# A graph layer kernel: dense products with their sides swapped, hop tables gathered in two float32r parts, 16 of 25 batches dense

## The chip, the cores and the metric

The kernel runs on one core of one Trainium2 chip. The metric is the device time of one execution in microseconds. Three executions took 3998.82, 3994.66 and 3999.19 us, the median is 3998.82 us. The engines are TensorE (PE in the rows; its weight loads are PEld), VectorE (DVE), ScalarE (ACT), GpSimd (POOL) and SyncE (SP, which here only issues transfers). They run at once and wait for each other through semaphores. A row such as L1175 names line 1175 of the kernel.

## The reference

There are 12500 nodes of 128 features and 212500 edges, sorted by destination: 100000 random pairs in both directions and a loop on each node.

```python
h = relu(layernorm(x))                            # per node
msg = where(edge_type == 0, h[src] @ W_data.T + b_data, h[src] @ W_control.T + b_control)
x = x + relu(segment_sum(msg, dst) + h @ W_self.T + b_self)
h = relu(layernorm(x))
norm = deg_inv_sqrt[src] * deg_inv_sqrt[dst]      # deg = edges into a node
y = h; total = h
for _ in range(2):                                # two hops
    y = segment_sum(y[src] * norm[:, None], dst)
    total = total + y
return x + total / 3
```

## The kernel before

**Nodes and edges.** The nodes are 98 blocks of 128, four blocks are a batch (512 nodes), so there are 25 batches. The edges are 208 groups of 8 chunks of 128 edges.

**The typed pass (k = 0).** A first stage makes a table of both kinds of messages for each node. Then the pass goes over all 208 groups. For each chunk GpSimd gathers 128 rows from the table in HBM (`gather`, L874), and VectorE makes a one-hot matrix of the destinations of the group (`make_hot`, L1465). TensorE multiplies both in fp32 (`sum_rows`, L1091), and VectorE adds the 128 rows of sums into a window of seven node blocks, in two parts where they straddle two blocks (`add_group`, L1487). When a batch is complete it is finished (`finish`): residual, layernorm, and the scaled rows that the first hop reads. They are stored as a table of fp32 rows of 512 bytes in HBM (`store_nodes`, L732). They are also kept in SBUF as two float32r parts (`table_parts`): the high part is ScalarE's copy (L982), the low part is what VectorE finds missing (L1413), so both together carry the fp32 value.

Beside it the pass makes count strips: for each of the first 60 destination blocks (15 batches) a matrix of how often each source node is linked to each destination. VectorE makes one-hot matrices (L1509 and L1512), four cells of edges at a time (a quad, 480 in all), in slots 24 to 205. TensorE multiplies them (L1135), ScalarE turns the counts into uint8 (L1002), SP stores them. TensorE also runs bf16 products that nobody reads (`fill`, L1126).

**The hops (k = 1, 2).** The first 15 batches are dense: their sums are the product of the count strips with the whole table in SBUF. The rest is sparse and goes as in the typed pass, with 82 groups per hop. A hop runs over slots. In slot i TensorE sums group i, then does its share of the dense steps (`dense_step`). A step is one tile (a block of 128 destinations) by one piece of 14 source blocks. It takes 14 products with the counts as the stationary side and 256 columns of the table (high and low part side by side) as the moving side (L1175). There are 60 x 7 = 420 steps per hop. The last slots of a pass already do steps of the next hop, the lead (`LEAD_TILES`). VectorE adds the two parts of each finished tile (`read_tile`, L1542).

The counts of a step come from HBM through a ring of seven places (`load_counts`, L772). ScalarE casts them from uint8 to float32r into a ring of three strips (`cast_counts`, L1011). SP issues the load of a place when the cast that used it is done, and it works in one fixed order: the loads of the slot's steps, then reloads, then stores of the batch that leaves, then the load of a batch that comes.

Gathers go through a ring of four places of 8 chunks (`RING`). At a hop's start GpSimd waits until the whole table is stored.

At the end of hop 1 the table in SBUF is replaced by the new one. SP reads 14 pieces of 7 blocks back (`reload`, L783), each when the last step that uses it is done and its batches are stored. ScalarE and VectorE split each again (L1016, L1413).

## Time and profile before

| | |
|---|---|
| median of three executions | 3998.82 us |
| the profiled execution, first to last instruction (its span) | 3997.9 us |
| around the span, against the median | 0.9 us |
| busy in the span: PE, PEld | 3405.9 us (85%), 2729.2 us (68%) |
| busy in the span: POOL, ACT, DVE | 2879.8 us (72%), 2329.7 us (58%), 2186.3 us (55%) |
| moved in the span | 571.77 MB, mean 143 GB/s |

The profiled execution has no time of its own beside the span. The page also shows the span in 40 slices. In the slices of the typed pass PE is busy 0.7 to 0.8, DVE 0.8 and the DMA engines 0.3. In those of the hops PE is busy 0.9 or more, DVE 0.2 and the DMA engines 0.6. Shares are means over stages with different limits, so each stage is read from its own rows. Matmuls are pipelined, so the mean time of one row (285 ns) is longer than the distance from one to the next.

### The profile page before, as it was taken

The numbers are of one execution on the slowest core, as the hardware profiler recorded it, in microseconds if no ns is written. First come the engines' busy times: TensorE is split into PE (matmuls) and PEld (weight loads), VectorE is DVE, ScalarE is ACT, GpSimd is POOL, SyncE is SP. The second block draws the span as 40 slices with busy tenths as digits, with TensorE's granted clock in tenths as the row PEclk, the third lists the DMA queues.
The fourth block names the chain that finished last, engine by engine and source line by source line (L and its number), as shares of the span: only waits on it lengthen the run. The fifth ranks groups of instructions, "written<-read, shape, count | busy, mean of one in ns | idle before, by whom it ended". The sixth has DMA issues, their size and how long they took to land.

```text
span 3997.9 us, 62254 instructions
## 1 busy us (share of the span) xinstructions
PE 3405.9 (85%) x23420; PEld 2729.2 (68%) x23420; DVE 2186.3 (55%) x3333; ACT 2329.7 (58%) x3075; POOL 2879.8 (72%) x3058
## 2 busy tenths in 40 slices
PE   7666777777777787777777899999998899999999
PEld 4344444444444444444444799999998899999999
DVE  7523888888888888888888422222222222222222
ACT  4001444444444444444444688888887788888887
POOL 2677777777777777777777577777776477777775
PEclk9788998999999999999999999999999999999999
DMA  6222333333333334333333566666666666666665
GB/s 194 85 61 61 109 119 121 113 109 110 126 109 110 114 110 128 110 109 125 110 115 112 170 179 187 192 192 187 189 189 184 179 179 176 187 182 181 179 184 145
DMA packets 367268, 571.77 MB, mean 143 GB/s; under 512 B 66678, under 2 KB 308225, under 8 KB 359283
## 3 DMA queue, kind: packets, MB, share of 16 engines
q1 hardware_dynamic: 270435, 370.74, 29.6%
q0 software_dynamic: 95664, 196.60, 19.2%
q8 instruction: 188, 3.08, 0.3%
q14 instruction: 117, 0.96, 0.1%
q10 hardware_dynamic: 864, 0.39, 0.0%
HBM read 424.48 MB, written 142.99 MB: 142 GB/s over the span
## 4 chain that ended last, share of the span: by engine, by line
PE 44%; POOL 38%; issue 13%; DVE 2%; DMA 2%; ACT 1%; SPq 0%; DVEq 0%; POOLq 0%; ACTq 0%
POOL rows L874 38%; PE wide L1175 34%; PE sums_bank L1091 7%; PE wide L1056 1%; ACT strip_ring L1011 1%; DMA stage<-hop_table 1%; DMA rows<-typed_table,index 0%; PE turned_bank L1126 0%; DVE big L1214 0%; DVE rows L1254 0%; DVE stage L1512 0%; POOL stage L914 0%; PE wide L1135 0%; DMA stage<-strips 0%; DMA big<-in_x 0%
## 5 line engine op out<-in xcount | busy, mean ns | idle before, releaser
L874 POOL DMA_INDIRECT rows<-typed_table,index x1661 | 1589.0, 957 | 506.0 <-issue 505.0
L874 POOL DMA_INDIRECT rows<-hop_table,index x1306 | 1251.9, 959 | 481.4 <-issue 394.9
L1011 ACT CAST strip_ring<-stage 128x1792 fp32r<-128x1792 uint8 x840 | 1409.2, 1687 | 285.3 <-PE wide L1175 279.2
L1175 PE MATMUL wide<-table_parts,strip_ring 128*128 128x256 f32 x11760 | 1461.0, 285 | 35.7 <-ACT strip_ring L1011 35.7
L1175 PEld LDWEIGHTS wide<-table_parts,strip_ring 128*128 128x128 f32 x11760 | 1431.3, 193 | 38.0 <-ACT strip_ring L1011 17.5
L1002 ACT CAST stage<-wide 128x392 uint8<-128x392 f32 x1920 | 790.3, 502 | 983.9 <-PE wide L1135 982.6
L1126 PE MATMUL turned_bank<-all_twos 128*128 128x512 bf16 x3328 | 1112.0, 394 | 0.0
L1091 PE MATMUL sums_bank<-rows,hot 128*128 128x129 f32 (+1 forms) x5934 | 801.2, 292 | 287.0 <-DMA rows<-typed_table,index 272.6
L1091 PEld LDWEIGHTS sums_bank<-rows,hot 128*128 128x128 f32 x5934 | 764.4, 206 | 337.8 <-issue 304.0
L1512 DVE TENSOR_TENSOR stage<-count_up,stage 128x1568 bf16<-128x1568 f32 x480 | 855.4, 1782 | 0.0
L1135 PE MATMUL wide<-stage 128*128 128x392 bf16 x1920 | 652.6, 340 | 221.8 <-DVE stage L1512 220.0
L1487 DVE SCALAR_TENSOR_TENSOR sums<-sums_bank,in_upper,sums 128x129 f32 (+1 forms) x372 | 129.8, 349 | 1064.8 <-PE sums_bank L1091 1042.6
L1126 PEld LDWEIGHTS turned_bank<-all_twos 128*128 128x128 bf16 x3328 | 339.0, 102 | 344.6 <-issue 53.5
L1135 PEld LDWEIGHTS wide<-stage 128*128 128x128 bf16 x1920 | 191.9, 100 | 460.2 <-DVE stage L1512 317.5
L1465 DVE TENSOR_TENSOR hot<-count_up,local 128x1024 f32<-128x1024 f32 x372 | 451.8, 1215 | 0.1
L1509 DVE TENSOR_TENSOR stage<-count_up,stage 128x512 bf16<-128x512 f32 x480 | 328.2, 684 | 174.2 <-PE wide L1135 174.0
L1542 DVE TENSOR_REDUCE own_in<-wide 128x128 f32<-128x256 f32 x120 | 50.8, 423 | 356.9 <-PE wide L1175 356.9
L976 ACT ACTIVATE batch_spread<-batch_spread 128x8 f32<-128x8 f32 x25 | 5.4, 216 | 249.6 <-DVE batch_spread L1225 249.6
L1487 DVE SCALAR_TENSOR_TENSOR sums<-sums_bank,base_all,sums 128x129 f32 (+1 forms) x372 | 127.8, 343 | 0.4
L1056 PE MATMUL wide<-stage,rows 128*128 128x384 f32 x196 | 78.5, 528 | 0.0
L1413 DVE TENSOR_TENSOR table_parts<-stage,table_parts 128x896 fp32r<-128x896 f32 x14 | 15.3, 1092 | 73.6 <-ACT table_parts L1016 73.6
L1402 DVE SCALAR_TENSOR_TENSOR xin<-scaled,xin 128x512 f32<-128x512 f32 (+1 forms) x50 | 34.2, 684 | 37.9 <-ACT scaled L945 35.1
(141 smaller groups left out, 669.5 us busy)
## 6 DMA issues: line engine op xcount, KB each, us to landing
stage<-strips SPq DMA_DIRECT2D x840, 224.0 KB
strips<-stage SPq DMA_DIRECT2D x60, 1568.0 KB
rows<-typed_table,index POOLq DMA_INDIRECT x1661
rows<-hop_table,index POOLq DMA_INDIRECT x1306
resid<-xin SPq DMA_DIRECT2D x50, 256.0 KB, 3.0
hop_table<-scaled SPq DMA_DIRECT2D x50, 256.0 KB, 3.8
xin<-resid SPq DMA_DIRECT2D x50, 256.0 KB
typed_table<-rows SPq DMA_DIRECT2D x49, 256.0 KB, 2.1
```

What stands on the lines that cost most here:

```text
L874: pool.indirect_dma_start(out=rows[:, o % RING, c, 0:P], out_offset=None, in_=tables[k], in_offset=bass.IndirectOffsetOnAxis(ap=index[:, c ...
L1002: act.copy(count_strips[tile % 2][:, :, w * CELL:(w + 1) * CELL], wide[:, nth % CELL_BANKS, 0:real_blocks * CELL].rearrange("p (b n) -> p ...
L1011: act.copy(strip_ring[:, number % STRIP_RING], counts_ring[place]).then_inc(strip_cast, 1)
L1056: last = pe.matmul(wide[:, i % 2 * PAIR + b, 0:KINDS * P], normed_t[i % 2][:, b * P:(b + 1) * P], w_all[:, :], start=True, stop=True)
L1091: last = pe.matmul(sums_bank[:, bank, 0:columns], hots[:, c, :], rows[:, slot, c, 0:columns], start=(c == 0), stop=(c == size - 1))
L1126: pe.matmul(turned[:, 0:4 * P].rearrange("p (n f) -> p n f", n=4), all_twos[:, :], all_twos[:, :].unsqueeze(1).to_broadcast([P, 4, P]), st ...
L1135: pe.matmul(wide[:, nth % CELL_BANKS, 0:real_blocks * CELL], quad_low[quad % 2][:, w, :], quad_hot[quad % 2][:, w, :], start=True, stop=Tr ...
L1175: last = pe.matmul(wide[:, nth % 4, 0:PARTS * P], strip_ring[:, number % STRIP_RING, b - first, :], table_parts[:, b, :, :].rearrange("p n ...
L1465: dve.tensor_tensor(hot[:, place, :, :], counting(CHUNKS, P), local[:, group * CHUNKS:(group + 1) * CHUNKS].unsqueeze(2).to_broadcast([P, ...
L1487: last = dve.scalar_tensor_tensor(out=into, in0=sums_bank[:, o % 2, 0:columns], scalar=inside_tile, in1=into, op0=ALU.mult, op1=ALU.add)
L1509: dve.tensor_tensor(quad_low[place], counting(QUAD, P), cell_low[:, cells].unsqueeze(2).to_broadcast([P, QUAD, P]), ALU.is_equal)
L1512: dve.tensor_tensor(quad_hot[place], counting(QUAD, columns), cell_key[:, cells].unsqueeze(2).to_broadcast([P, QUAD, columns]), ALU.is_equ ...
```

## The change

**The sides are swapped.** A step is now one batch (four tiles) by one piece of 4 source blocks. The stationary side is one part of one table block, the moving side the counts of the four tiles, 512 columns. High and low part are two products that accumulate in the same bank, so the result is the sum of both already, but transposed: features by nodes. VectorE copies it out (`read_batch`), TensorE turns it with four transposes (`turn_batch`), and `finish` reads the turned bank. There are 25 pieces (the last has two blocks) and 400 steps per hop.

**The counts** are loaded for two steps at a time, four tiles by 8 blocks, into a ring of three such loads.

**The hop tables** hold 256 words per row, the high and the low part, and are stored by two transfers. For hop 2's table, too, ScalarE now makes the high part (into the first words of `index`) and VectorE the low part. Both wait in the queue: ScalarE's copy also waits for the table stores of the previous batch, and the store waits for `low_ready`. The gathers fetch 1 KB rows into a ring of three places. The one-hot matrices of the hops are float32r, a chunk is one product of 256 columns, and VectorE adds the two halves one after the other. The reload writes both parts straight into the SBUF table.

**16 batches are dense**: 64 tiles, 512 quads in the same slots, 73 groups per hop, the dense steps in 71 slots.

```diff
-DENSE_BATCHES = 15
+DENSE_BATCHES = 16
 DENSE_TILES = DENSE_BATCHES * NODE_BLOCKS
 PAIR_TILES = 9
 PARTS = 2
-STEP_BLOCKS = 14
-COUNT_RING = 7
+STEP_BLOCKS = 4
+LOAD_STEPS = 2
+COUNT_RING = 3
 STRIP_RING = 3
 RELOAD_BLOCKS = 7
-RELOAD_RING = 3
 RELOADS_AT_ONCE = 3
 STAGE_WORDS = 11264
-DENSE_SLOTS = 80
-LEAD_TILES = 3
-LEAD_AT_ONCE = 3
+DENSE_SLOTS = 71
+LEAD_BATCHES = 1
+LEAD_AT_ONCE = 4
...
+        strip_ring = sbuf("strip_ring", [STRIP_RING, NODE_BLOCKS, STEP_BLOCKS, P], F32R)
+        row_words = HOP_RING * CHUNKS * PARTS * P - RING * CHUNKS * TILE
+        assert STRIP_RING * piece_words + COUNT_RING * count_words + row_words <= STAGE_WORDS
+        sbuf("rest_of_stage", [STAGE_WORDS - STRIP_RING * piece_words - row_words])
+        hop_rows = sbuf("hop_rows", [HOP_RING, CHUNKS, PARTS * P], F32R)
+        hop_hot = sbuf("hop_hot", [HOT_RING, CHUNKS, P], F32R)
...
-            def store_nodes(n, k, s):
+            def store_nodes(n, k, s, even):
                 if k < HOPS:
                     sp.wait_ge(resid_ready, n + 1)
                     sp.dma_start(of_batch(resid, s), in_blocks(xin[:, n % XIN, :])).then_inc(resid_stored[n % XIN], 16)
-                    sp.wait_ge(scaled_ready, n + 1)
-                    sp.dma_start(of_batch(tables[k + 1], s), in_blocks(scaled[:, n % 2, :])).then_inc(table_stored[n % 2], 16)
+                    nodes = slice(s * BATCH, s * BATCH + held(s) * P)
+                    sp.wait_ge(low_ready, n + 1)
+                    for part, values in enumerate((high_of(k, s, even), low_of(n, k, s, even))):
+                        sp.dma_start(tables[k + 1][nodes, part * P:(part + 1) * P].rearrange("(b p) f -> p b f", p=P),
+                                     values.bitcast(F32)).then_inc(table_stored[n % 2], 16)
...
+                def load_counts(n):
+
+                    k, j = divmod(n, loads_per_hop)
+                    q, part = counts_orders[k + 1][j]
+                    covered = pieces_of_counts(part)
+                    first, end = blocks_of_piece(covered[0]).start, blocks_of_piece(covered[-1]).stop
+                    place = n % COUNT_RING
+                    if n >= COUNT_RING:
+                        sp.wait_ge(strip_cast, end_of_counts[n - COUNT_RING] + 1)
+                    sp.dma_start(counts_ring[place][:, :, 0:(end - first) * P],
+                                 strips[q * NODE_BLOCKS:(q + 1) * NODE_BLOCKS, :, first:end, :].rearrange("t p b n -> p t (b n)")
                                  ).then_inc(counts_in[place], 16)
...
+                def reload(piece):
                     for s in reload_batches(piece):
                         n = event_of[1][s]
-                        sp.wait_ge(table_stored[n % 2], 16 * count_of(n + 1, 2, n % 2))
+                        sp.wait_ge(table_stored[n % 2], 32 * count_of(n + 1, 2, n % 2))
                     sp.wait_ge(strip_used, last_step_with(piece) + 1)
-                    if r >= RELOAD_RING:
-                        sp.wait_ge(reload_low, r - RELOAD_RING + 1)
                     first = piece * RELOAD_BLOCKS
-                    sp.dma_start(in_blocks(reloaded[r % RELOAD_RING], RELOAD_BLOCKS),
+                    sp.dma_start(table_parts[:, first:first + RELOAD_BLOCKS, :, :].rearrange("p b n f -> p b (n f)").bitcast(F32),
                                  tables[2][first * P:(first + RELOAD_BLOCKS) * P, :].rearrange("(b p) f -> p b f", p=P)
-                                 ).then_inc(reload_in[r % RELOAD_RING], 16)
+                                 ).then_inc(reload_in[piece], 16)
 
                 def load_counts_behind(numbers):
                     for number in numbers:
-                        if number + COUNT_RING < HOPS * steps_per_hop:
-                            load_counts(number + COUNT_RING)
+                        n = counts_of_step[number]
+                        if number == end_of_counts[n] and n + COUNT_RING < HOPS * loads_per_hop:
+                            load_counts(n + COUNT_RING)
...
-                    pool.wait_ge(summed, o - RING + 1)
+                    pool.wait_ge(summed, o - RING + 1 if o < groups else max(groups, o - HOP_RING + 1))
...
+                if k < HOPS:
+                    blocks = held(s)
                     act.wait_ge(scaled_ready, n + 1)
-                    act.copy(table_parts[:, first:first + blocks, 0, :], in_blocks(scaled[:, n % 2, 0:blocks * P], blocks)).then_inc(high_ready, 1)
+                    if n and not (k == 0 and even):
+                        act.wait_ge(table_stored[(n - 1) % 2], 32 * count_of(n, 2, (n - 1) % 2))
+                    act.copy(high_of(k, s, even), in_blocks(scaled[:, n % 2, 0:blocks * P], blocks)).then_inc(high_ready, 1)
...
+                    n = counts_of_step[number]
+                    _, _, _, piece = step_at(number)
+                    columns = len(blocks_of_piece(piece)) * P
+                    ahead = piece % LOAD_STEPS * STEP_BLOCKS * P
+                    act.wait_ge(counts_in[n % COUNT_RING], 16 * (n // COUNT_RING + 1))
                     if number >= STRIP_RING:
                         act.wait_ge(strip_used, number - STRIP_RING + 1)
-                    act.copy(strip_ring[:, number % STRIP_RING], counts_ring[place]).then_inc(strip_cast, 1)
-
-                def part_high(r, piece):
-                    first = piece * RELOAD_BLOCKS
-                    act.wait_ge(reload_in[r % RELOAD_RING], 16 * (r // RELOAD_RING + 1))
-                    act.copy(table_parts[:, first:first + RELOAD_BLOCKS, 0, :], in_blocks(reloaded[r % RELOAD_RING], RELOAD_BLOCKS)
-                             ).then_inc(reload_high, 1)
+                    act.copy(strip_ring[:, number % STRIP_RING].rearrange("p t b n -> p t (b n)")[:, :, 0:columns],
+                             counts_ring[n % COUNT_RING][:, :, ahead:ahead + columns]).then_inc(strip_cast, 1)
...
+            def sum_rows(k, bank, slot, size, place):
+                columns = TILE if k == 0 else PARTS * P
                 for c in range(size):
-                    last = pe.matmul(sums_bank[:, bank, 0:columns], hots[:, c, :], rows[:, slot, c, 0:columns],
+                    hots, values = (hot, rows) if k == 0 else (hop_hot, hop_rows)
+                    last = pe.matmul(sums_bank[:, bank, 0:columns], hots[:, place, c, :], values[:, slot, c, 0:columns],
                                      start=(c == 0), stop=(c == size - 1))
                 return last
...
+                    for b in blocks:
+                        for part in range(PARTS):
+                            last = pe.matmul(wide[:, nth % 4, 0:BATCH].rearrange("p (t n) -> p t n", t=NODE_BLOCKS),
+                                             table_parts[:, b, part, :], strip_ring[:, number % STRIP_RING, :, b - blocks.start, :],
+                                             start=(begins and b == blocks.start and part == 0),
+                                             stop=(ends and b == blocks[-1] and part == PARTS - 1))
                     last.then_inc(strip_used, 1)
+
+                def turn_batch(k, q):
+
+                    nth = nth_product(k, q)
+                    pe.wait_ge(batch_read, nth + 1)
+                    if nth:
+                        earlier = (k, q - 1) if q else (k - 1, DENSE_BATCHES - 1)
+                        pe.wait_ge(fresh_made, event_of[earlier[0]][earlier[1]] + 1)
+                    for b in range(NODE_BLOCKS):
+                        last = pe.transpose(turned[:, b * P:(b + 1) * P], own_in[:, q % 2, b * P:(b + 1) * P], identity[:, :])
+                    last.then_inc(batch_turned, 1)
...
+                dve.wait_ge(scaled_ready, n + 1)
+                dve.wait_ge(high_ready, n + 1)
+                dve.tensor_tensor(low_of(n, k, s, even), in_blocks(values, blocks), high_of(k, s, even).bitcast(F32), ALU.subtract
+                                  ).then_inc(low_ready, 1)
...
+                    for part in range(PARTS if k else 1):
+                        if part:
+                            last.then_inc(high_added, 1)
+                            dve.wait_ge(high_added, o - groups + 1)
+                        for n, inside_tile in enumerate((in_upper[:, group:group + 1], in_lower[:, group:group + 1])):
+                            into = flat_sums[:, ds(base - tile_place(first) + n * TILE, columns)]
+                            last = dve.scalar_tensor_tensor(out=into, in0=sums_bank[:, o % 2, part * P:part * P + columns], scalar=inside_tile,
+                                                            in1=into, op0=ALU.mult, op1=ALU.add)
                     last.then_inc(added, 1)
...
+                def read_batch(k, q):
+                    nth = nth_product(k, q)
+                    dve.wait_ge(strip_used, step_number(k, batch_last[k][q]) + 1)
+                    earlier = nth_product(k, q - 2) if q >= 2 else (nth_product(k - 1, max(s for s in range(DENSE_BATCHES) if s % 2 == q % 2))
+                                                                    if k > 1 else -1)
+                    if earlier >= 0:
+                        dve.wait_ge(batch_turned, earlier + 1)
+                    dve.tensor_copy(own_in[:, q % 2, :], wide[:, nth % 4, 0:BATCH]).then_inc(batch_read, 1)
```

On TensorE, in the middle of a hop, the order before has at the border of two slots a step's products, the sum of a group from `rows` and `hot`, and the next step:

```order
L1175 MATMUL wide<-table_parts,strip_ring 128x256 [waits strip_cast]
L1175 MATMUL wide<-table_parts,strip_ring 128x256 x13
L1091 MATMUL sums_bank<-rows,hot 128x128 [waits rows_landed0,added,hot_ready]
L1091 MATMUL sums_bank<-rows,hot 128x128 x7
L1175 MATMUL wide<-table_parts,strip_ring 128x256 [waits strip_cast]
```

After the change, at such a border, with the result of a batch in `own_in` to be turned:

```order
L1217 MATMUL wide<-strip_ring,table_parts 128x512 [waits strip_cast]
L1217 MATMUL wide<-strip_ring,table_parts 128x512 x7
L1131 MATMUL sums_bank<-hop_rows,hop_hot 128x256 [waits hop_rows_landed0,added,hot_ready]
L1131 MATMUL sums_bank<-hop_rows,hop_hot 128x256 x7
L1231 MATMUL turned_bank<-identity,own_in 128x128 [waits fresh_made,batch_read]
L1231 MATMUL turned_bank<-identity,own_in 128x128 x3
L1217 MATMUL wide<-strip_ring,table_parts 128x512 [waits strip_cast]
```

A step of 14 products of 256 columns became one of 8 products of 512 columns with the names on the input side exchanged, the sum has 256 columns, and the turn stands ahead of the slot's dense steps and waits for VectorE's copy and for the finishing of the batch before it.

On SyncE, where the first reloads of hop 1's end begin, the order before is this (`stage` holds counts and reloaded rows, `strips` the counts in HBM):

```order
L772 DMA stage<-strips 128x1792 [waits strip_cast] x10
L730 DMA resid<-xin 128x4x128 [waits resid_ready]
L732 DMA hop_table<-scaled 128x4x128 [waits scaled_ready]
L772 DMA stage<-strips 128x1792 [waits strip_cast] x5
L783 DMA stage<-hop_table 128x7x128 [waits strip_used,table_stored0,table_stored1]
L783 DMA stage<-hop_table 128x7x128 [waits table_stored1,strip_used,table_stored0]
L783 DMA stage<-hop_table 128x7x128 [waits table_stored1,strip_used]
```

And after:

```order
L811 DMA stage<-strips 128x4x1024 [waits strip_cast] x3
L821 DMA table_parts<-hop_table 128x7x256 [waits strip_used,table_stored0,table_stored1]
L821 DMA table_parts<-hop_table 128x7x256 [waits table_stored1,strip_used,table_stored0]
L763 DMA resid<-xin 128x4x128 [waits resid_ready]
L767 DMA hop_table<-index 128x4x128 [waits low_ready]
L767 DMA hop_table<-scaled 128x4x128
L811 DMA stage<-strips 128x4x1024 [waits strip_cast] x3
```

The reload goes to `table_parts` with rows of 256 words, the table is stored by two transfers behind the wait for `low_ready`, and a slot sends three loads of counts where it sent five. Each reload still waits for `strip_used` ahead of the next counts.

## Rows read from the trace of the kernel before

**Rows 1.** Timeline: where the dense products of each hop begin (start, duration).

```profile
2240.74 10.31 PE L1175 MATMUL wide<-table_parts,strip_ring 128*128 128x256 f32 x84 [0.75 <-ACT strip_ring L1011]
...
3127.79 13.74 PE L1175 MATMUL wide<-table_parts,strip_ring 128*128 128x256 f32 x98 [7.07 <-ACT strip_ring L1011]
```

**Rows 2.** Stretches: length, busy (instructions) per engine, granted clock, DMA share, GB/s.

```profile
2240.70:3127.80 887.10, 859.22 (x7187) 857.98 (x7187) 233.92 (x427) 716.35 (x437) 628.37 (x653) 0.99 0.66 186
3127.80:3997.90 870.10, 855.23 (x7186) 854.53 (x7186) 212.83 (x388) 704.70 (x421) 623.58 (x653) 0.99 0.63 177
300.00:2150.00 1850.00, 1419.78 (x7795) 852.49 (x7793) 1514.49 (x2036) 805.66 (x1958) 1402.02 (x1471) 0.92 0.36 112
2400.00:3000.00 600.00, 600.00 (x5074) 600.00 (x5074) 158.75 (x287) 495.54 (x296) 455.38 (x475) 1.00 0.67 189
3045.00:3127.80 82.80, 58.99 (x444) 58.07 (x443) 28.08 (x40) 49.02 (x37) 28.59 (x28) 0.88 0.64 173
...
10.00:30.00 20.00, 14.84 (x47) 8.76 (x48) 13.81 (x55) 10.70 (x29) 0.00 (x0) 1.00 1.06 304
```

**Rows 3.** The chain that ended last, inside hop 1 (start, duration).

```profile
2604.40 1.78 PE sums_bank L1091 x16
2606.18 8.39 PE wide L1175 x70
```

**Rows 4.** Groups by form, 300 to 2150 us: busy, mean ns, idle before.

```profile
L874 POOL DMA_INDIRECT rows<-typed_table,index x1456 | 1388.5, 954 | 443.7 <-issue 442.8 <-PE sums_bank L1091 0.9
L1126 PE MATMUL turned_bank<-all_twos 128*128 128x512 bf16 x2908 | 993.0, 392 | 0.0
L1512 DVE TENSOR_TENSOR stage<-count_up,stage 128x1568 bf16<-128x1568 f32 x460 | 819.8, 1782 | 0.0
...
L1509 DVE TENSOR_TENSOR stage<-count_up,stage 128x512 bf16<-128x512 f32 x460 | 314.6, 684 | 165.1 <-PE wide L1135 164.9
...
L914 POOL DMA_INDIRECT stage<-edge_pairs,cell_first x15 | 14.4, 962 | 4.6 <-issue 4.6
...
L982 ACT CAST table_parts<-scaled 128x512 fp32r<-128x512 f32 x21 | 13.0, 617 | 28.6 <-DVE scaled L1404 28.6
...
L1153 PE MATMUL wide<-identity,stage 128*128 128x128 f32 x30 | 5.8, 277 | 0.0
```

**Rows 5.** Groups by form, both hops.

```profile
L1175 PE MATMUL wide<-table_parts,strip_ring 128*128 128x256 f32 x11760 | 1461.0, 285 | 35.7 <-ACT strip_ring L1011 35.7
...
L1011 ACT CAST strip_ring<-stage 128x1792 fp32r<-128x1792 uint8 x839 | 1407.6, 1687 | 285.3 <-PE wide L1175 279.2 <-DMA stage<-strips 6.1
L874 POOL DMA_INDIRECT rows<-hop_table,index x1306 | 1251.9, 959 | 481.4 <-issue 394.9 <-DMA hop_table<-scaled 83.5 <-PE sums_bank L1091 3.1
...
L1487 DVE SCALAR_TENSOR_TENSOR sums<-sums_bank,in_upper,sums 128x128 f32 x164 | 57.5, 351 | 862.2 <-PE sums_bank L1091 861.9 <-issue 0.3
```

**Rows 6.** Transfers issued, 2400 to 3000 us: KB each, median us to landing.

```profile
stage<-strips SPq DMA_DIRECT2D x295, 224.0 KB
rows<-hop_table,index POOLq DMA_INDIRECT x475
resid<-xin SPq DMA_DIRECT2D x17, 256.0 KB, 3.5
```

**Rows 7.** Timeline: fillers and casts one behind the other.

```profile
2229.05 3.62 PE L1126 MATMUL turned_bank<-all_twos 128*128 128x512 bf16 x16
...
2238.91 9.62 ACT L1011 CAST strip_ring<-stage 128x1792 fp32r<-128x1792 uint8 x6
```

**Rows 8.** Hop 1's end: three pieces of the chain, then a gather of the timeline.

```profile
3053.80 4.87 DMA stage<-hop_table
...
3071.41 6.20 DMA stage<-hop_table
3077.82 0.66 issue
...
3058.27 1.65 POOL L874 DMA_INDIRECT rows<-hop_table,index  x1 [0.30 <-issue]
```

More of the change, by code:

```diff
@@ L161, in gnn_kernel, with blocks_of_piece, pieces_of_counts @@
-    lead_steps, orders = zip(*([(0, [])] + [order_of_steps(k) for k in range(1, HOPS + 1)]))
-    assert all(len(orders[k]) == steps_per_hop for k in range(1, HOPS + 1))
+    pieces = -(-real_blocks // STEP_BLOCKS)
+    loads = -(-pieces // LOAD_STEPS)
+    steps_per_hop = DENSE_BATCHES * pieces
+    loads_per_hop = DENSE_BATCHES * loads
+    def blocks_of_piece(piece):
+        return range(piece * STEP_BLOCKS, min((piece + 1) * STEP_BLOCKS, real_blocks))
+    def pieces_of_counts(part):
+        return range(part * LOAD_STEPS, min((part + 1) * LOAD_STEPS, pieces))
@@ new lines, in parts_of_batch, with order_of_counts @@
+    def parts_of_batch(s):
+        return {block // (STEP_BLOCKS * LOAD_STEPS) for block in range(s * NODE_BLOCKS, min((s + 1) * NODE_BLOCKS, real_blocks))}
+    last_of_pass = [{total - 1}, {total - 1, DENSE_BATCHES - 1}]
+    def order_of_counts(k):
+        late = set().union(*(parts_of_batch(s) for s in last_of_pass[k - 1]))
+        lead = [(q, part) for q in range(LEAD_BATCHES) for part in range(loads) if part not in late]
+        order = lead + [(q, part) for q in range(LEAD_BATCHES) for part in sorted(late)]
+        order += [(q, part) for q in range(LEAD_BATCHES, DENSE_BATCHES) for part in range(loads)]
+        return sum(len(pieces_of_counts(part)) for _, part in lead), order
@@ new lines, in gnn_kernel @@
+    lead_steps, counts_orders = zip(*([(0, [])] + [order_of_counts(k) for k in range(1, HOPS + 1)]))
+    orders = [[(q, piece) for q, part in order for piece in pieces_of_counts(part)] for order in counts_orders]
+    assert all(len(orders[k]) == steps_per_hop and len(counts_orders[k]) == loads_per_hop for k in range(1, HOPS + 1))
+    counts_of_step = [n for k in range(1, HOPS + 1) for n, (_, part) in enumerate(counts_orders[k], (k - 1) * loads_per_hop)
+                      for _ in pieces_of_counts(part)]
@@ L499, in table_need @@
         def table_need(k):
[L501 removed]
+            return [32 * count_of(k * total, 2, parity) for parity in range(2)]
         def event_at(k, slot):
@@ L534, in step_at, with dense_at, nth_product @@
             return k + 1, j, *orders[k + 1][j]
-        def tiles_done_in(k, i):
-            return [t for t in range(DENSE_TILES) if tile_slot[k][t] == i]
+        def dense_at(k, slot):
+            return [s for at, s in events[k] if at == slot and is_dense(k, s)]
+        def nth_product(k, q):
+            return (k - 1) * DENSE_BATCHES + q
         TURN, PLACE, FETCH, CELLS_TURN, CELLS_AHEAD = 2, 4, 10, 2, 6
```

206 lines of the change are left out of this document (85 added, 121 removed).

## The prediction

> **What bounds the kernel now.** I read the timeline for where the parts begin, the chain of waits inside a hop, the stretches, the groups by form, the transfers, and at last the end of hop 1. The span has three parts: the typed pass up to 2240.7 us, hop 1 to 3127.8 us and hop 2 to the end [rows 1, 2]. Up to 2240.7 us GpSimd's gathers set the pace: one is 0.954 us and 0.30 us of issue follows, 1850 us hold 1456 of them and 15 of the cells' (1471 x 1.257 = 1849 us), and GpSimd waited for sums 0.9 us in all [rows 2, 4]. In the hops TensorE does: it is busy 600.00 of 600 us, and the chain is nothing but 8.39 us of dense products (five steps of 14) and 1.78 us of the sum of one group, 10.17 us a slot [rows 2, 3]. The reader should also see how near the others are: eight gathers at 0.959 + 0.30 us are 10.0 us of that slot, ScalarE's casts wait only for TensorE, and the DMA engines are busy 0.67 [rows 2, 5, 6].
>
> So per hop: 420 x 14 = 5880 dense products at 8.39/70 = 119.9 ns, 705.0 us, and 653 chunks in two passes each at 1.78/16 = 111.3 ns, 145.3 us. Together 850.3 us. Hop 1 lasts 887.1 us, 36.8 more; hop 2 870.1 us, 19.8 more [rows 2]. The executed median, 3998.8 us, is 0.9 us above the span of 3997.9 us, and I add that 0.9 at the end.
>
> **The dense products.** The change turns 5880 products of 256 columns per hop into 16 x 98 x 2 = 3136 of 512 columns. The columns do not fall: 5880 x 256 = 1.505 million become 3136 x 512 = 1.606 million, since the 16th batch adds a fifteenth. What can fall is what a product costs above its columns. At 2.4 GHz (the clock is granted 1.00 here [rows 2]) 256 columns are 106.7 ns, so 13.2 ns of the 119.9 are something else. No row shows a float32r product of 512 columns. The bounds: the bf16 fillers of 512 columns follow each other after (3.62 - 0.39)/15 = 215 ns [rows 4, 7], which gives 674 us; and if the 13.2 ns grow with the columns, it is 2 x 119.9 = 239.8 ns and 752 us. I take one constant per product, 213.3 + 13.2 = 226.5 ns, 710.5 us, which lies between them: the fp32 sums of the same loop, whose pass of 128 columns takes 111.3 ns, also stand a constant 4.6 ns above 106.7.
>
> The Trainium skill ("TensorE: Matmul & The Clock Gate", Back-to-back issue gap) gives N/2.4 + 2.5 ns for an isolated product, 216 ns at 512 columns. The trace agrees for bf16 (215 ns), and disagrees at 256 float32r columns (109 by the rule, 119.9 measured); the same section's sustained 131 ns at 512 columns is not what this trace shows. By the rule hop work would be 34 us less than mine, which is the first rival below.
>
> **The sums.** 72 groups of 8 chunks and one of 5, 581 chunks, each now one pass of 256 float32r columns. That is exactly the form of today's dense product, so 119.9 ns: 69.7 us in place of 145.3. **The turns**: 16 x 4 transposes, between 0.111 and 0.277 us each [rows 3, 4]; at 0.17 they are 11 us (7 to 18). TensorE per hop: 710.5 + 69.7 + 11 = 791 us, 59 less than 850.3, and 118 for both.
>
> **What could stand in the way beside it.**
> - GpSimd: a gather's row grows from 512 B to 1 KB. The gather of cells already takes 1 KB rows, and costs 0.962 us against 0.954 [rows 4]. So 581 x 1.26 = 732 us per hop, hidden behind 791. The ring has three places in place of four; GpSimd is then up to two groups ahead, 20 us, and a row lands in a few us.
> - ScalarE: 384 casts of 2048 elements and 16 of 1024. Unhindered, six casts of 1792 took 9.62 us, (9.62 - 1.69)/5 = 1.59 apart [rows 7]. In proportion 1.81 us, 710 us per hop; by the mean of one, 1.687 [rows 5], it is 1.93 us and 757 us. Hop 1 adds 25 copies of the high part at about 0.62 [rows 4], 15 us. Hidden, by 20 us at the worse end.
> - ScalarE's copy also waits for the previous batch's table stores. Six of hop 1's events lie one slot after another; there the stores go out only behind that slot's counts, and a store lands after 3.5 us [rows 6]. ScalarE is up to three strips ahead, so I charge 1 to 2 us for each, 10 us (0 to 25). Behind the waiting copy stand the next casts, and behind VectorE's wait the next group's sums, which have a slot to spare.
> - VectorE is busy 159 of 600 us [rows 2]: two more additions of 0.35 us a slot [rows 5], and 0.7 us of reading a batch, are hidden.
> - Typed pass: 512 instead of 480 quads of 0.684 + 1.782 us are 79 us more on VectorE in 182 slots, 0.43 us in a slot of 10.06, where it is busy 0.82 [rows 2, 4]. GpSimd still sets the pace. I charge 4 us (0 to 20). Splitting and storing the table twice is hidden but for the last batch, where it adds a copy, a subtraction and a store, about 2 us in all.
> - Hop 1's end: TensorE is busy 59 of 82.8 us. SP waits until a piece of the table is used, sends the reloads, and the next counts come behind them (4.87 and 6.20 us of transfer, then ScalarE's copy, then a cast) [rows 2, 8]. The change takes the copies and subtractions away, but doubles the bytes: 14 x 896 KB, 42 us at 304 GB/s [rows 2], in the same place of SP's queue, behind a counts ring of six steps instead of seven. I expect the gain and the loss to be equal, and keep the 36.8 us (20 less to 30 more).
>
> **The sum**: 3997.9 - 118 + 10 + 4 + 2 + 0.9 = 3897 us.
>
> **Rivals.**
> 1. The pace is that of the bf16 fillers. TensorE would need 755 us per hop, 72 less in all, 3825. But then the casts (710 to 757 us, and 15 in hop 1) and the gathers (732) lie beside it with no room, and I give back 14 us per hop: 3853. For it: the constant may be a weight load that 512 columns hide. Against it: nothing in the rows says where the 13.2 ns come from.
> 2. The excess grows with the columns, 239.8 ns: 833 us per hop, 3980, still 0.5% faster. For it: the excess is larger with 256 columns (13.2 ns) than with 128 (4.6 ns in the sums' passes).
> 3. The transfers decide, and it gets slower. Hop 1 moves 103 MB of counts, 76 of rows (today 43), 25 x 1 MB for the events and 13 of reloads, 217 MB in 840 us: 258 GB/s. Today a share of 0.67 moves 189, which extrapolates to 282, and the best 20 us moved 304 [rows 2]. The place is the counts ring: three loads of 512 KB. A load goes out when the one three before it is cast, so 208 loads take 208 x (L + 3.6)/3, L from issue to landing. TensorE needs one every 3.80 us; it decides from L = 7.8 us. A store of 256 KB lands after 3.5 us, a reload of 448 KB after 4.9 to 6.2 [rows 6, 8], and an event puts up to 1 MB in front. At L = 9 us a hop takes 874 us: 3897 + 166 = 4063. Against it: that L is reached around an event, not in each of the 208. The Trainium skill ("DMA: Bandwidth & Descriptors", Where 436 GB/s comes from) puts the HBM side near 358 GB/s, more room than any stretch of this trace shows.
> 4. Gathers get longer under that load: one took 1.65 us beside reloads [rows 8]. GpSimd takes over from 791/581 = 1.36 us a gather; at 1.40 it is 813 us per hop, 3941.
> 5. The change does not do what it says: if one float32r pass of the sums cost what two take today, 2 x 111.3 ns, 60 us per hop return and it is 4016.
>
> **How the numbers follow.** My forecast 0.50, rival 1 0.20, rival 2 0.13, rival 3 0.10, rival 4 0.05, rival 5 0.02. About 0.2% (8 us) is what can be told from no change. Forecast, rivals 1 and 2 and most of 4 lie further below 3991 than that; I leave 0.04 for no change (between rivals 2 and 3), 0.12 for slower, 0.84 for faster. The range runs from rival 1 without its give-back, 3825, to 3995, where rival 2 with 15 us of waits for events ends; rival 3 is left out. The forecast's own range, from the waits' bounds, is 3860 to 3950.
>
> **What would show it.** Per form: the products of 512 columns (3136 per hop, their chain time over their count near 226 ns), the sum of eight chunks near 0.96 us against 1.78, TensorE still busy nearly all of hop 2's middle, the casts near 1.8 us apart when free, GpSimd's gather near 0.96 us with waits for sums. The slot should be near 10.8 us. Wrong would be: waits of casts for counts through the whole hop (rival 3), waits of sums for rows (rival 4), a chain pace of 215 or 240 ns, or a typed pass that ends more than 20 us later.

## The result, and the profile after

The changed kernel took 3892.82 us in the median of four executions (3889.46 to 3900.65), the kernel before 3999.01 us beside it on the same chip (3994.66 to 4001.44). The ratio is 0.9734, with an interval of 0.9723 to 0.9746. The forecast was 3897 us. The profiled execution took 3894.17 us, its span is 3892.4 us. Busy time of each engine in it, from the page (before, PE was busy 3405.9 us and POOL 2879.8):

```profile
PE 3314.4 (85%) x16748; PEld 2354.8 (60%) x16748; DVE 2290.2 (59%) x3557; ACT 2417.2 (62%) x3174; POOL 2742.7 (70%) x2915
```

Timeline of TensorE, where hop 1 and hop 2 begin (start, duration, idle time before), as [rows 1]:

```profile
2244.21 14.88 PE L1217 MATMUL wide<-strip_ring,table_parts 128*128 128x512 f32 x64
...
3091.83 38.37 PE L1217 MATMUL wide<-strip_ring,table_parts 128*128 128x512 f32 x160 [12.24 <-ACT strip_ring L1055]
```

The typed pass ends 3.5 us later than before, hop 1 is 39.5 us shorter (847.6 for 887.1), hop 2 69.5 us shorter (800.6 for 870.1). Stretches, with the columns of [rows 2]: hop 1, hop 2, the typed pass, hop 1's middle and its end.

```profile
2244.20:3091.80 847.60, 804.82 (x3783) 673.14 (x3782) 252.17 (x513) 730.58 (x428) 560.98 (x581) 0.98 0.83 253
3091.80:3892.40 800.60, 791.48 (x3781) 666.59 (x3781) 224.12 (x459) 718.20 (x401) 552.95 (x581) 0.99 0.81 244
300.00:2150.00 1850.00, 1443.98 (x7920) 847.55 (x7919) 1582.08 (x2101) 862.64 (x2082) 1402.26 (x1470) 0.92 0.38 118
2300.00:2960.00 660.00, 645.05 (x3063) 541.73 (x3062) 206.70 (x410) 586.66 (x342) 477.10 (x494) 0.99 0.84 255
2960.00:3091.80 131.80, 105.72 (x482) 86.92 (x481) 36.63 (x74) 90.09 (x54) 62.95 (x66) 0.91 0.88 272
```

In hop 2 TensorE is still busy in 791.5 of 800.6 us, so it sets the pace as before. In hop 1 it is idle for 42.8 us, 14.9 of them in the middle, where before it was busy in 600.00 of 600. In hop 1 the DMA engines went from a share of 0.66 to 0.83.

A piece of the chain in hop 2 (start, duration), to be laid beside [rows 3]:

```profile
3504.19 0.44 PE turned_bank L1231 x4
3504.63 9.09 PE wide L1217 x40
3513.72 0.95 PE sums_bank L1131 x8
3514.68 9.10 PE wide L1217 x40
```

Forty products take 9.10 us, 227.5 ns each. Eight chunks of a sum take 0.955 us, 119.4 ns each, where sixteen passes took 1.78. A turn of a batch takes 0.44 us.

Groups by form in both hops, with the columns of [rows 5]:

```profile
L1217 PE MATMUL wide<-strip_ring,table_parts 128*128 128x512 f32 x6272 | 1467.7, 393 | 42.8 <-ACT strip_ring L1055 42.7
L1055 ACT CAST strip_ring<-stage 128x2048 fp32r<-128x2048 uint8 x768 | 1408.4, 1903 | 137.3 <-PE wide L1217 114.6 <-DMA stage<-strips 20.8 <-issue 1.5
...
L913 POOL DMA_INDIRECT hop_rows<-hop_table,index x1162 | 1113.9, 959 | 521.7 <-issue 333.7 <-PE sums_bank L1131 83.8 <-DMA hop_table<-scaled 65.6
...
L1023 ACT CAST index<-scaled 128x512 fp32r<-128x512 f32 x24 | 14.7, 614 | 44.2 <-DMA hop_table<-scaled 44.2
```

The gather of 1 KB rows costs GpSimd the same 959 ns as that of 512 B rows in [rows 5], and GpSimd now waits 83.8 us for sums: it has room, though little. The last row is the one that matters below: ScalarE waited 44.2 us for stores of the table.

Transfers from 2400 to 2900 us (count, KB, median us to landing), with [rows 6], and the transfers in the chain of hop 1's end, with [rows 8]:

```profile
stage<-strips SPq DMA_DIRECT2D x115, 512.0 KB, 4.4
...
resid<-xin SPq DMA_DIRECT2D x15, 256.0 KB, 5.1
...
hop_table<-scaled SPq DMA_DIRECT2D x15, 256.0 KB, 5.8
```

```profile
3027.07 9.24 DMA stage<-strips
3042.77 10.61 DMA stage<-strips
3058.39 8.72 DMA stage<-strips
3082.93 6.26 DMA hop_table<-scaled
```

A load of `resid` lands after 5.1 us, before it was 3.5. Counts land after 4.4 us in the middle and after 9 to 11 us behind the reloads of hop 1's end.

### The profile page after: what moved, and what is told of

It reads as the page before. It is cut to its first block, busy times and chain, and to the rows that moved or that the text cites. A ratio compares the mean times of both kernels' runs of the same rounds, so it can differ in the third digit from the quotient of the medians.

```text
span 3892.4 us, 48593 instructions
## 1 busy us (share of the span) xinstructions
PE 3314.4 (85%) x16748; PEld 2354.8 (60%) x16748; DVE 2290.2 (59%) x3557; ACT 2417.2 (62%) x3174; POOL 2742.7 (70%) x2915
## 4 chain that ended last, share of the span: by engine, by line
PE 40%; POOL 39%; issue 13%; DVE 3%; DMA 3%; ACT 2%; SPq 0%; DVEq 0%; POOLq 0%; ACTq 0%
POOL rows L913 38%; PE wide L1217 34%; PE sums_bank L1131 4%; ACT strip_ring L1055 2%; DMA stage<-strips 1%; PE wide L1094 1%; DMA hop_table<-scaled 1%; DVE stage L1571 0%; DMA rows<-typed_table,index 0%; PE turned_bank L1166 0%; DVE big L1270 0%; DVE rows L1310 0%; POOL stage L953 0%; PE turned_bank L1231 0%; PE wide L1175 0%
## 5 line engine op out<-in xcount | busy, mean ns | idle before, releaser
L1055 ACT CAST strip_ring<-stage 128x2048 fp32r<-128x2048 uint8 (+1 forms) x800 | 1438.9, 1869 | 139.5 <-PE wide L1217 116.8
L1217 PE MATMUL wide<-strip_ring,table_parts 128*128 128x512 f32 x6272 | 1467.7, 393 | 42.8 <-ACT strip_ring L1055 42.7
L913 POOL DMA_INDIRECT hop_rows<-hop_table,index x1162 | 1113.9, 959 | 521.7 <-issue 333.7
L1217 PEld LDWEIGHTS wide<-strip_ring,table_parts 128*128 128x128 f32 x6272 | 1176.2, 189 | 287.3 <-ACT strip_ring L1055 31.3
L1546 DVE SCALAR_TENSOR_TENSOR sums<-sums_bank,in_upper,sums 128x128 f32 (+1 forms) x500 | 174.1, 348 | 951.6 <-PE sums_bank L1131 922.5
L1131 PE MATMUL sums_bank<-rows,hot 128*128 128x129 f32 x3322 | 468.9, 300 | 207.2 <-DMA rows<-typed_table,index 191.9
L1131 PEld LDWEIGHTS sums_bank<-rows,hot 128*128 128x128 f32 x3322 | 446.7, 213 | 253.1 <-issue 213.8
L1520 DVE TENSOR_TENSOR hot<-count_up,local 128x1024 f32<-128x1024 f32 x208 | 252.0, 1212 | 0.1
L1520 DVE TENSOR_TENSOR hop_hot<-count_up,local 128x1024 fp32r<-128x1024 f32 x146 | 177.1, 1213 | 0.0
L1546 DVE SCALAR_TENSOR_TENSOR sums<-sums_bank,base_all,sums 128x128 f32 (+1 forms) x500 | 170.8, 342 | 0.5
```

What stands on the lines that cost most here:

```text
L913: pool.indirect_dma_start(out=into, out_offset=None, in_=tables[k], in_offset=bass.IndirectOffsetOnAxis(ap=index[:, chunk:chunk + 1], axis ...
L1055: act.copy(strip_ring[:, number % STRIP_RING].rearrange("p t b n -> p t (b n)")[:, :, 0:columns], counts_ring[n % COUNT_RING][:, :, ahead: ...
L1131: last = pe.matmul(sums_bank[:, bank, 0:columns], hots[:, place, c, :], values[:, slot, c, 0:columns], start=(c == 0), stop=(c == size - 1))
L1217: last = pe.matmul(wide[:, nth % 4, 0:BATCH].rearrange("p (t n) -> p t n", t=NODE_BLOCKS), table_parts[:, b, part, :], strip_ring[:, numbe ...
L1520: dve.tensor_tensor((hot if o < groups else hop_hot)[:, place, :, :], counting(CHUNKS, P), local[:, group * CHUNKS:(group + 1) * CHUNKS].u ...
L1546: last = dve.scalar_tensor_tensor(out=into, in0=sums_bank[:, o % 2, part * P:part * P + columns], scalar=inside_tile, in1=into, op0=ALU.mu ...
```

## The experiments

Where nothing else is said, an edit is made to the changed kernel, and ratios are against the kernel before on the same chip.

**1. What a product costs above its columns.** Each product of 512 columns is issued as two, of 256 and 256 and of 384 and 128. The edit for the second, with `start` at the first and `stop` at the last product of a bank (the first has `((0, 2), (2, NODE_BLOCKS))`):

```diff
-                             last = pe.matmul(wide[:, nth % 4, 0:BATCH]..., table_parts[:, b, part, :], strip_ring[..., :, b - blocks.start, :],
+                             for lo, hi in ((0, 3), (3, NODE_BLOCKS)):
+                                 last = pe.matmul(wide[:, nth % 4, lo * P:hi * P]..., table_parts[:, b, part, :], strip_ring[..., lo:hi, b - blocks.start, :],
```

> The changed kernel with every dense product of 512 columns made as two of 256 with the same stationary side. Theory (a constant of 12 to 13 ns per float32r product): two products take 2 x 119.9 = 239.8 ns against 227.5, 12.3 x 3136 = 39 us per hop, about 3970 us. Rival (the excess goes with the columns, and the 119.9 ns of the kernel before came from its layout): 113.8 ns each, about 3893 us.

> The changed kernel with every dense product of 512 columns made as one of 384 and one of 128 with the same stationary side. Constant per product: 12.3 ns + 0.42 ns a column gives 173.7 + 66.1 = 239.8 ns, about 3970 us, as with two of 256. Rival (a product is never shorter than the load of its weights, which the fp32 sums bound at 111 ns): 173.7 + 111 = 285 ns and more, 57 x 3136 = 179 us per hop, about 4250 us.

The halves took 3961.84 us (0.9904, 0.9884 to 0.9924), near the 3970 of a constant per product. The uneven pair took 4242.41 us (1.0605, 1.0584 to 1.0627), where the constant alone gave 3970 and the rival 4250, so the rival holds. The chain of each in hop 2:

```profile
3512.17 9.60 PE wide L1218 x80
```

```profile
3517.80 11.42 PE wide L1218 x80
```

A product of 256 columns takes 9.60/80 = 120.0 ns, just as in the kernel before, so from 256 to 512 columns a product is 12.4 ns and 0.420 ns a column (107.5 ns more for 256 columns more). That gives 173.7 ns for 384 columns. The pair took 2 x 142.75 = 285.5 ns, so the product of 128 columns took 112 ns, not 66, if that of 384 takes what the line gives (no run has it alone). The constant of the prediction holds for 256 and 512 columns and fails at 128, where something of 112 ns decides. The Trainium skill ("TensorE: Matmul & The Clock Gate", LDWEIGHTS) gives 128/1.2 = 107 ns for loading 128 columns of weights; the 112 ns here are near it. That it is the weight load was not tried by itself, and no run has a product of 128 columns alone.

**2. How much the 16th batch moves.** The changed kernel with 15 dense batches, and the kernel before with 16:

```diff
-DENSE_BATCHES = 16
+DENSE_BATCHES = 15
...
-DENSE_SLOTS = 71
+DENSE_SLOTS = 80
```

> The changed kernel with 15 dense batches again (82 groups per hop, dense steps in 80 slots). Theory: with sides swapped and float32r sums TensorE needs only 2940 x 227.5 ns + 653 x 119.4 ns + 7 us = 754 us per hop, so GpSimd's 653 gathers at 1.25 us, 816 us, and some 30 us until the first are there, set the pace: about 3950 us, sums wait for rows. Rival (DMA or ScalarE bound, which fall with the dense share): below 3893.

> The kernel before with 16 dense batches (73 groups per hop, dense steps in 71 slots) and nothing else changed. TensorE needs 6272 x 119.9 ns + 581 x 222.5 ns = 881 us per hop against 850: about 4060 us. If GpSimd had been the hidden bound of the kernel before, it would be below 3999.

With 15 batches the changed kernel took 3971.78 us (0.9931, 0.9911 to 0.9951), 79 us more than with 16. A piece of its chain in hop 2, 20 us by line, then gather and issue in turn:

```profile
by line: POOL hop_rows L913 80.4%; issue 24.4%
...
3499.25 0.95 POOL hop_rows L913
3500.20 0.30 issue
```

The dense products (`wide` L1217) are gone from the chain: TensorE would need 754 us per hop, but 653 gathers at 1.26 us are 823. The forecast of 3950 was 22 us too low: GpSimd stood idle 37.6 and 41.8 us ahead of the hops' first gathers, until the table was stored, where 30 each were charged. The kernel before with 16 batches took 4066.69 us (1.0168, 1.0148 to 1.0189), 68 us slower, and its chain alternates these two:

```profile
3499.92 1.78 PE sums_bank L1091 x16
3501.70 10.07 PE wide L1175 x84
```

There TensorE was the bound, and 392 products more at 119.9 ns against 72 chunks fewer at 222.5 are 31 us per hop. The same move pays 79 us in the one kernel and costs 68 in the other.

**3. What the float32r sums give.** The hops' sums take the high part alone, as fp32 in two passes of 128 columns; the low part's sum and its addition are left out.

```diff
-                    last = pe.matmul(sums_bank[:, bank, 0:columns], hots[:, place, c, :], values[:, slot, c, 0:columns],
+                    weights_now, moving = ... (hop_hot[:, place, c, :].bitcast(F32), hop_rows[:, slot, c, 0:columns].bitcast(F32))
+                    last = pe.matmul(sums_bank[:, bank, 0:columns], weights_now, moving,
```

> The changed kernel with the sums of the hops made from the high part alone, read as fp32, 128 columns in two passes as in the kernel before (the low part of the sparse rows is left out, and VectorE's second addition with it). Theory: a chunk costs 2 x 111.3 ns instead of 119.4, 60 us more per hop, about 4013 us. Rival (float32r sums only trade TensorE's time for VectorE's and the transfers'): below 3960.

It took 4002.13 us (1.0008, 0.9998 to 1.0018): with 16 dense batches the whole gain is gone. Its chain in hop 2:

```profile
3508.32 9.10 PE wide L1218 x40
3517.42 1.79 PE sums_bank L1132 x16
```

The sum is back at 1.79 us and the products stay at 9.10. 581 chunks at 222.5 - 119.4 ns more are 120 us in two hops; 109 came. In the profiled executions TensorE is busy 117 us longer in the two hops (1713.0 for 1596.3), but idle 11.7 us less (40.2 for 51.9), and the typed pass ends 3.8 us earlier. Why it is idle less was not tried.

**4. Is the ring of counts near its limit?** 

```diff
-COUNT_RING = 3
+COUNT_RING = 2
```

> The changed kernel with a counts ring of two loads instead of three. The prediction's ring model: a load takes (L + 3.6)/2 with L = 4.4 us to landing, 4.0 us, where TensorE needs one every 3.8: some 40 us per hop, about 3970 us, and casts wait for counts. Rival (loads land long before they are needed): within 10 us of 3893.

It took 4036.43 us (1.009, 1.007 to 1.0111), 144 us more than with three places, against an expected 77. The chain in hop 2:

```profile
3505.00 3.94 DMA stage<-strips
3508.93 0.02 issue
3508.95 1.52 ACT strip_ring L1055
3510.47 0.29 issue
3510.76 1.91 ACT strip_ring L1055
3512.67 0.02 issue
3512.69 4.66 DMA stage<-strips
```

A load of counts, two casts, the next load into the same place: a circle of 7.7 us here and 8.4 in the next turn. Hop 2 lasts 863.8 us (3171.5 to 4035.3) for 208 loads, 4.15 us each, so two places turn in 8.3 us. By the prediction's rule (L + 3.6)/2 that is L = 4.7 us, the mean of the chain's three landings (3.94, 4.66 and 5.52). So the rule fits, and L was larger than I had put in. The fit is looser than it looks: from 3180 to 4000 us the chain is 35% products, 30% loads of counts and 24% casts, so the ring sets the pace in a part of the hop alone, and three landings are few. With three places it decides from 7.8 us, and the changed kernel's L is 4.4 in the middle: rival 3 fails by that margin, and it is a real limit at hop 1's end, where L is 9 to 11.

**5. The waits for table stores.** In the middle of hop 1 a copy of the high part into `index` stands on ScalarE and waits until the previous batch's copy has been stored. The chain around one of the six (start, duration):

```profile
2630.71 1.92 ACT strip_ring L1055
...
2632.64 0.36 SPq L811
...
2633.05 1.03 SPq L763
...
2634.12 0.51 SPq L767
...
2634.66 6.67 DMA hop_table<-scaled
...
2641.41 0.04 ACT index L1023
...
2641.93 1.90 ACT strip_ring L1055
...
2643.88 8.13 PE wide L1217 x25
```

SPq is SP's time for sending a transfer. SP sends the next load of counts (L811) only when the cast at 2630.71 is done, then `resid` (L763), then the stores (L767); the store takes 6.67 us. Behind the waiting copy stand the next casts, and TensorE is idle for 5.05 us. On its timeline, forty products ahead of that wait and the forty behind it:

```profile
2628.62 9.26 PE L1217 MATMUL wide<-strip_ring,table_parts 128*128 128x512 f32 x40
...
2643.88 11.53 PE L1217 MATMUL wide<-strip_ring,table_parts 128*128 128x512 f32 x40 [5.05 <-ACT strip_ring L1055]
```

The edit gives the copy a second place in `index`:

```diff
-        high_hop = index[:, 0:BATCH].bitcast(F32R)
+        high_hop = [index[:, p * BATCH:(p + 1) * BATCH].bitcast(F32R) for p in range(2)]
...
-                    if n and not (k == 0 and even):
+                    if n and not even:
```

> The changed kernel with two places for the high part of hop 1's batches (1024 free words of index instead of 512), so that ScalarE's copy no longer waits for the previous batch's table stores. Theory (ScalarE's wait behind the stores stalls TensorE): ScalarE waited 44.2 us in six places, TensorE stood idle 14.3 us in 2400 to 2960 us and 4.6 and part of 12.2 us at hop 1's end; these go, about 3870 us (3862 to 3880), and no copy waits for a table store. Rival (TensorE's idle time there comes from late counts): 3888 to 3893 us, and the idle time stays under another name.

It took 3865.12 us (0.966, 0.9644 to 0.9676), 28 us less than the changed kernel. Its stretches hop 1 and hop 1's middle:

```profile
2246.80:3063.80 817.00, 796.99 (x3784) 668.70 (x3782) 251.97 (x513) 731.00 (x428) 560.04 (x581) 0.99 0.86 262
2300.00:2960.00 660.00, 659.93 (x3168) 555.53 (x3167) 213.31 (x423) 607.19 (x353) 492.75 (x512) 1.00 0.86 263
```

TensorE is busy in 659.93 of 660 us. Hop 1 is 30.6 us shorter: 22.8 us of idle time are gone (42.8 to 20.0), and 7.8 us of busy time for the same instructions (804.82 to 796.99). The latter goes with the clock. In the changed kernel, ahead of the wait, the 6.1 us behind it, and after these:

```profile
2620.00:2637.00 17.00, 17.00 (x80) 14.24 (x79) 4.93 (x9) 14.02 (x9) 12.06 (x13) 1.00 0.77 218
...
2643.88:2650.00 6.12, 6.12 (x17) 4.90 (x18) 3.75 (x8) 5.45 (x3) 4.11 (x5) 0.62 0.57 145
2650.00:2660.00 10.00, 10.00 (x49) 8.42 (x48) 2.95 (x6) 8.99 (x6) 2.75 (x3) 1.00 0.87 265
```

The granted clock falls to a mean of 0.62, most of it at the lower level of 1.2 GHz, after 5 us of idle time, and the forty products behind the wait take 11.53 us on the timeline in place of 9.26. This wait of 5 us cost 7.3. The other waits of the middle show that the loss has no fixed size: behind one of 4.86 us the products lost 2.6 us, behind one of 2.27 us 1.7, and behind one of 2.14 us 0.2.

**6. Hop 1's end.** On top of experiment 5, the reloads go out from GpSimd behind its last gather of hop 1 instead of from SP among the counts; or at most two of them at a time instead of three; or counts are loaded a step at a time; or the last two together.

```diff
+                    if o == first_of[2]:
+                        for _, piece in reload_order:
+                            reload(piece)
```

```diff
-RELOADS_AT_ONCE = 3
+RELOADS_AT_ONCE = 2
```

```diff
-LOAD_STEPS = 2
-COUNT_RING = 3
+LOAD_STEPS = 1
+COUNT_RING = 6
```

> two_high with the 14 reloads at hop 1's end issued from GpSimd, behind its last gather of hop 1, instead of SP. Theory (the counts come late because they are queued on SP behind the wait for strip_used and the reloads): TensorE's idle 18 us between 3008 and 3064 us shrink to a few, about 3852 us (3845 to 3860). Rival (the 16 engines are full there, share 0.92, whoever issues): 3860 us or more, and the wait moves to the reloaded table or the next hop's rows.

> two_high with at most two reloads in a slot instead of three. Theory (the counts wait behind the reloads in SP's queue): a stall of 5 to 6 us there loses the 2.7 us of one reload of 896 KB, about 3857 us. Rival (the bytes are the same and the stretch is full, as pool_reload showed): 3862 to 3868 us.

> two_high with the counts loaded one step at a time into a ring of six (the same bytes and the same space as three of two steps). Theory (at hop 1's end a load is late by what the ring does not cover): a load then has five steps of slack instead of four, 1.8 us more at each of the four stalls there, about 3858 us. Rival (rows of 512 B instead of 1 KB cost the transfer engines more than the slack gives): 3866 us or more.

> two_high with at most two reloads in a slot and the counts loaded one step at a time into a ring of six. Theory (both cut the same four stalls at hop 1's end, 12.9 us of idle TensorE in two_high_reload_2, of which 6.2 us lie behind the last group's sums and no counts): the other 6.7 us lose 3 to 5, about 3852 us. Rival (512 B rows raise the share of the transfer engines, 0.93 in fine_ring, and give back what the slack wins): 3855 us or more.

The changed kernel itself ran again beside the second and the third:

> The changed kernel once more, beside the next two on the same chip: 3893 us (3889 to 3901).

| kernel | median us (lowest to highest) | ratio to before |
|---|---|---|
| changed kernel again | 3893.99 (3891.8 to 3897.92) | 0.9744 (0.9727 to 0.976) |
| reloads from GpSimd | 3867.34 (3865.4 to 3869.7) | 0.9668 (0.9652 to 0.9684) |
| two reloads at a time | 3855.62 (3853.35 to 3858.29) | 0.9644 (0.9628 to 0.9661) |
| counts a step at a time | 3861.07 (3857.09 to 3861.6) | 0.9655 (0.9639 to 0.9671) |
| both of these | 3858.01 (3853.88 to 3859.78) | 0.964 (0.9624 to 0.9656) |

With the reloads on GpSimd, the timeline of TensorE at hop 1's end has these waits:

```profile
3049.33 5.82 PE L1217 MATMUL wide<-strip_ring,table_parts 128*128 128x512 f32 x16 [6.20 <-ACT strip_ring L1055]
...
3072.64 27.53 PE L1217 MATMUL wide<-strip_ring,table_parts 128*128 128x512 f32 x109 [13.37 <-ACT strip_ring L1055]
```

The waits for counts are gone and one of 13.37 us has come. Its cast stands behind ScalarE's copy of the high part, and that copy behind 17.28 us in which VectorE waits ahead of the next batch's finishing (L1451); the profile names no releaser for them. The waiting was moved, not removed; the forecast of 3852 failed and the rival's time (3860 or more) holds, though the wait moved to the last batches' finishing and not where the rival had it. The 140 us around the end of hop 1 with three reloads at a time and then with two, both with the second place in `index`:

```profile
2960.00:3100.00 140.00, 121.63 (x538) 100.15 (x536) 36.57 (x72) 106.97 (x65) 53.99 (x56) 0.93 0.92 286
```

```profile
2960.00:3100.00 140.00, 127.06 (x576) 105.20 (x575) 38.93 (x76) 114.11 (x69) 59.58 (x63) 0.95 0.97 302
```

TensorE is idle 5.4 us less and gets 38 more instructions through, and the time is near the 3857 forecast. The medians differ by 9.5 us (3865.12, 3855.62), on two chips, and the intervals of the ratios overlap, so the size of this step is not settled. A last wait of 6.2 us is left ahead of hop 2's lead. In the version with two reloads at a time its chain runs from TensorE's last sum at 3045.75 us over VectorE's additions and the finishing of the last batch (to 3050.39) and a cast of 1.90 us to the next product at 3052.97. In the changed kernel it is 12.24 us, with a store of the table of 6.26 in its chain: the second place in `index` removes that too. The version with two reloads at a time has the lowest median, 37 to 38 us below the changed kernel and 144 below the one before. A finer ring gives nothing on top of it that can be told: 3858 us with both, where 3852 was forecast and the rival had 3855 or more. By itself it fell between forecast (3858) and rival (3866); TensorE's waits at hop 1's end, without the last of 6.2, add up to 11.3 us with it and to 12.0 in experiment 5.

## Why the prediction was right

**The dense products** (710.5 us per hop forecast): 3136 x 227.5 ns = 713.4. One constant per product was the right rule, and rivals 1 (215 ns) and 2 (239.8 ns) fall, both by a row: 227.5 in the chain. Of the two reasons I gave for it, one was no evidence. I read the fp32 passes of 128 columns (111.3 ns) as 106.7 ns and a constant, but 106.7 ns are 256 columns at 2.4 GHz, and I had no row that gives them to 128. The passes stand near the 112 ns of experiment 1, so they may be under that other limit; no run shows it.

The Trainium skill ("TensorE: Matmul & The Clock Gate", Back-to-back issue gap) has 216 ns for an isolated product of 512 columns. The trace disagrees for float32r, with 227.5, as it did at 256 columns.

**The sums** (69.7 us): 581 x 119.4 ns = 69.4. Rival 5 falls, and experiment 3 shows that with 16 dense batches there is no gain without this step. With 15 it need not be so: by these prices TensorE would need 668.9 + 145.3 + 7.0 = 821 us per hop with fp32 sums, 29 less than before, beside 823 of gathers. That is an estimate, and no run has it. **The turns** (11 us): 64 x 0.11 = 7.0; I had taken a middle value where the lower end held. TensorE per hop is 789.8 us, forecast 791, before 850.3.

**Where the 60.5 us per hop come from.** For 15 batches the swap takes 5880 x 119.9 ns to 2940 x 227.5, 36.2 us less. The sums take 653 chunks from 222.5 to 119.4 ns, 67.3 less. The 16th batch adds 196 products (44.6) and takes 72 chunks away (8.6), 36.0 more. The turns add 7.0. By TensorE alone the 16th batch should not be there; it pays because 653 gathers would last 823 us (experiment 2).

**GpSimd and rival 4**: the gather of 1 KB rows is 959 ns, as forecast; it did not lengthen at a DMA share of 0.83. **ScalarE**: eight free casts took 14.51 us, (14.51 - 1.90)/7 = 1.80 us apart, forecast 1.81. **The typed pass**: 3.5 us later, forecast 4 and 2.

**The waits for table stores** are the term that was mis-sized: I charged 10 us, within 0 to 25, and taking them away gave 28 (experiment 5), more than my upper bound. The six places were right. I had the store land after 3.5 us, as `resid` did before, and it takes 5.8 and more at the new DMA share, and I did not count the clock that falls after the wait.

**Hop 1's end**: I kept the 36.8 us that hop 1 had over TensorE's work and added the 10. It is now 847.6 - 789.8 = 57.8, 11 more than the 46.8 forecast; with the second place in `index` it is 817.0 - 789.8 = 27.2. So the waits for stores took 30.6 in place of 10, and what else hop 1 loses fell from 36.8 to 27.2. Hop 2 has 10.8 in place of the 19.8 that I kept, 9 less: before, TensorE waited for counts three times in hop 2's first 40 us (2.35, 0.45 and 4.34 us), and now the profile shows no such wait in hop 2. The two errors together are 2 us, so by luck the total of 3897 is closer than its terms deserve. The forecast's own range, too, was added up loosely: the bounds of its waits, typed pass and hop 1's end give 3863 to 3958, not 3860 to 3950.

**Rival 3** had the right place and formula: a ring with two places fits it, as far as experiment 4 can tell. Three places keep L at 4.4 us, below 7.8, but for hop 1's end. It had the engines full near 282 GB/s; hop 1 moved 253 at a share of 0.83, and experiment 6 has 302 at 0.97.

## What to carry to other kernels

Price an instruction by a constant and a slope from rows of at least two sizes, and look for a floor below the smaller: here 12.4 ns + 0.420 ns a column for float32r from 256 to 512 columns, but 112 ns at 128. Where a buffer is written from by a store and refilled by an engine whose queue feeds the bottleneck, price the wait at the landing time under the new load, and add the lowered clock behind it; a second buffer of 2 KB a partition was worth more than a quarter of the whole change. And a move of work between two near bounds (here the 16th batch) has no price of its own: it cost 68 us in the one kernel and paid 79 in the other.

## What the runs showed of the hardware that I had not expected

- A float32r product of 128 columns takes 112 ns, hardly less than one of 256 (119.9 ns), if one of 384 takes the 173.7 of the line (experiment 1).
- The TensorE wait of 5.05 us in experiment 5 is followed by 6 us at a granted clock of 0.62, and costs 7.3 us in all.
- With counts in rows of 512 B the DMA engines are busier than with rows of 1 KB for the same rate. The two kernels of experiments 6 and 5, 2400 to 2600 us, share and GB/s last:

```profile
2400.00:2600.00 200.00, 200.00 (x962) 168.65 (x961) 65.24 (x129) 184.75 (x109) 151.18 (x157) 1.00 0.93 264
```

```profile
2400.00:2600.00 200.00, 200.00 (x961) 168.58 (x960) 64.78 (x130) 185.78 (x108) 152.15 (x158) 1.00 0.87 266
```

The Trainium skill ("DMA: Bandwidth & Descriptors", Why small descriptors are slow) states a fixed cost of some three cycles per packet beside one cycle for 32 bytes. For the counts alone that is 38 cycles for 1 KB in place of 35, an estimate from that figure. The measured 0.93 for 0.87 goes the same way, but only a part of it lies in the counts: in these stretches the share of SP's queue, which has the counts, rises from 55.4% to 57.5%, and that of the gathers' queue from 31.4% to 34.8%, though their rows are the same.
